# A graph layer's message sums: three more batches of edges through dense counts, 23 fewer gathered groups

## The chip, the core and the metric

The kernel runs on one core of one Trainium2 chip. The metric is the device time of one execution in microseconds; the median of three runs of the kernel before is 1320.35 us (1319.23 to 1321.12).

## What is computed

One message-passing layer on 6250 nodes with 128 features and 206250 edges sorted by destination, each with one of three types:

```
h = relu(layernorm(x))
parts = [relu(h)]
for t in range(3):
    msg = relu(h[src] @ W_e[t].T + b_e[t])
    msg = where(edge_type == t, msg, 0)
    parts.append(segment_sum(msg, dst, 6250))
agg = concatenate(parts, axis=1)
for t in range(3):
    updated = where(node_type == t, agg @ W_n[t].T + b_n[t], updated)
out = x + updated + h
```

## The kernel before

**Table.** Messages depend on the source node and the type alone. So the first stage (up to about 78 us) computes, for each of 49 tiles of 128 nodes, all three messages of each node (`mm`, L705 and L707) and writes them to a table in HBM. What is left is a sum of table rows for each destination. Two ways of doing that run side by side.

**Gathered groups.** The first `E0` edges are cut into `GD` groups of 512. POOL fetches a group's 512 table rows by four indirect DMAs of 128 rows (L647) into one of six slots. VectorE builds a one-hot of destination and type (L1205), TensorE multiplies the rows by it (L770, four f32 matmuls of 27 columns, each two passes in the profile), and VectorE adds the sums to the accumulator `acc` (L1297). Groups are taken from the last to the first, one in each step.

**Dense batches.** The last `NW` = 2 × `BATCHES` rows of 1920 edges (15 tiles of 128) are not gathered. For each type and batch (`q` runs over 3 × `BATCHES` passes; a batch is two rows) TensorE first counts how often each source node occurs for each of 64 destination columns. That is a *build*: `count` (L791) multiplies one-hots of a source's low 7 bits (`lhot`, `lmid`, L1230 and L1225) by one-hots of its high bits and the destination column (`jhot`, `jmid`, L1216). A row's 15 tiles are done in three builds (`UNITS`), in seven pieces of the columns (`CUT`), each in a PSUM bank that ScalarE casts to f16 into `counts` (L957). Of 15 tiles, `D_OFF` gives the first column of each and `D_WID` its number of columns; a tile's destinations must lie in this window. A *product* (L807) then multiplies the counts by the table of that type, split into three bf16 parts ("planes"): seven products of seven 384-column matmuls for each pass. VectorE sums the three parts (L1318), TensorE transposes (L814), VectorE adds to `acc` (L1297).

**Finish.** A tile of 128 nodes whose sums are complete is multiplied by the node weights (L825 to L829) and stored.

**Order.** The steps are laid out when the kernel is built. `dealt` deals out builds and products evenly, by `SIZE` (3 for a product, 2, 2 and 3 for the builds, 9 for a finish), over steps 1 to `NS` − 7, where `NS` is the number of gathered groups. In each step TensorE does the gathered group, a finish if one is due, then its share of dense pieces. VectorE prepares the one-hots of step s + 1 in step s. POOL runs up to six groups ahead.

**What else the change touches.** `LEAD` rows ahead of the dense ones are loaded with them so that the number of rows is a multiple of 16 (L504), and are marked as empty (`far(e_typ)` in the POOL block). `SPLIT` gives the step at which each of seven groups of planes of the first type is split into its parts (`load_planes`, `plane_top`, `plane_rest`, `plane_low`); the products of that type wait for them. If any edge lies outside its window, `flag` is set and a branch at the end of the kernel recomputes all sums.

Of the kernel before, what the change touches and what calls it, by code (L numbers as in the profile page):

```python
# [24 lines left out]
PAD_SRC = 2666666  # L25
PAD_TYPE = -T * PAD_SRC

BATCHES = 23
BW = 2
WT = 15  # L30
WE = WT * P
LEAD = 2
SLOTS = 6
OFF = (0, 3, 9, 11)
WID = (8, 8, 7, 9)
WS = 9
MID = 9
WG = 20
D_OFF = (0, 4, 9, 13, 17, 21, 25, 29, 33, 37, 40, 44, 48, 51, 55)
D_WID = (9, 9, 7, 7, 7, 7, 6, 6, 6, 7, 8, 7, 8, 9, 9)  # L40
D_WS = 9
D_MID = 27
D_AT = (0, 7, 12)
ROUND = 12582912.0
SL = 64
CUT = (0, 10, 20, 29, 39, 48, 56, 64)
UNITS = ((0, 1), (2, 3), (4, 5, 6))
OWN = ((0, 1, 2, 3), (5, 6, 7, 8), (10, 11, 12, 13, 14))
CROSS = (4, 9)
# [13 lines left out]
def build(nc, x, src, dst, etype, ntype, w_e, b_e, w_n, b_n, out):  # L63
# [9 lines left out]
    TD = T * D  # L73
    NW = BATCHES * BW
    E0 = E - NW * WE
    LR = LEAD + NW
    GD = -(-E0 // GE)
    NS = GD
    SF = E0 // GE
    SR = E0 - SF * GE  # L80
    PIECES = len(CUT) - 1
    NQ = T * BATCHES
    NA = LEFT + NB * P + SL
# [8 lines left out]
    assert D == P and NR and ER and GF == G - 1 and NB == MC * 7 and NB == HB  # L92
    assert SF == GD - 1 and SR and LR <= HALF and LR % 16 == 0 and BW * SL <= 128 and max(D_WID) == D_WS and WT % 2 == 1
    assert HB * max(z - a for a, z in zip(CUT, CUT[1:])) <= 512 and CUT[-1] == SL
    assert 5 * EW <= T * NA and EW % 4 == 0 and OFF[-1] + WS == WG and D_OFF[-1] + D_WS == SL and T * JT < 2048
    assert LEFT >= D_MID and SLOPE * G * 1.0 <= N and P < GD <= 2 * P
# [10 lines left out]
    def group_at(s):  # L107
        return NS - 1 - s
# [31 lines left out]
    def touches(g, i):  # L140
        return SLOPE * g - SLACK - MID <= (i + 1) * P - 1 and SLOPE * g + AHEAD + WG > i * P

    def wide_touches(w, i):
        first = SLOPE / TPG * (E0 // P + w * WT)
        return first - SLACK - D_MID <= (i + 1) * P - 1 and first + AHEAD + SL > i * P


    def plan(hand):
        at = {i: s for s in range(D0, D1 + 1) for kind, i in hand[s] if kind == "prod"}
        last = [at[q * MC + MC - 1] for q in range(NQ)]  # L150
        wide_done = [last[NQ - BATCHES + w // BW] + 2 for w in range(NW)]
        ready = [max([s for s in range(NS) if touches(group_at(s), i)] + [wide_done[w] for w in range(NW) if wide_touches(w, i)])
# [46 lines left out]
        return [j for j in range(NB) if FIN[j] == s]  # L199


    SPLIT = (-1, -1, -1, 0, 0, 0, 2)

    def splits_at(s):
        return [m for m in range(MC) if SPLIT[m] == s]


    def kept_step(k):
        t, c = divmod(k, MC)
        a, z = (PROD_STEP[t * BATCHES * MC] if t else SPLIT[-1]) + 5, PROD_STEP[((t + 1) * BATCHES - 2) * MC]  # L210
        return a + (z - 6 - a) * c // (MC - 1)

    KEEP = [kept_step(k) for k in range((T - 1) * MC)]
    FETCH = [PROD_STEP[((k // MC + 1) * BATCHES - 1) * MC + k % MC] for k in range((T - 1) * MC)]

# [6 lines left out]
    with ExitStack() as ctx:  # L222
        def sb(name, shape, dt=F32):
            return ctx.enter_context(nc.sbuf_tensor(name, shape, dt))
# [18 lines left out]
        def far(a):  # L243
            return a[:, ES:EW]
# [10 lines left out]
        KEPT = [u for own in OWN for u in own]  # L255
        JW = HB * sum(D_WID[u] for u in KEPT)
        JAT = {u: HB * sum(D_WID[v] for v in KEPT if v < u) for u in KEPT}
        JB = max(AB, NB * D)
# [6 lines left out]
        lhot = sb("lhot", [P, len(KEPT), P], BF16)  # L265
        jmid = {u: sb(f"jmid{u}", [P, 2, HB * D_WID[u]], BF16) for u in CROSS}
        lmid = {u: sb(f"lmid{u}", [P, 2, P], BF16) for u in CROSS}
# [15 lines left out]
        col_s = sb("col_s", [1, -(-GD // 4) * 4], I32)  # L283
        col_d = sb("col_d", [1, BATCHES, 4], I32)
        flag = sb("flag", [1, 4], I32)
# [175 lines left out]
        def wide_keys(to, m):  # L461
            n = 2 * TPG
            b = (m - PAIR) // 2
            return (to[:, :, b * n:(b + 1) * n].rearrange("p w (c h) -> p c h w", h=2),
                    psE[m % 2][:, :].rearrange("p (c h w) -> p c h w", h=2, w=HALF)[:, :, :, LEAD:LR])

        def bank_of(i, p):
            return i // 3 * PIECES + p
# [8 lines left out]
        def _(sp):  # L477
# [20 lines left out]
            def dense_tiles(e0):  # L498
                return e0[E0 - LEAD * WE:E].rearrange("(w u j) -> w u j", u=WT, j=P)

# [104 lines left out]
        def _(pool):  # L605
# [10 lines left out]
                      allow_small_or_imprecise_dtypes=True).then_inc(consts, 1)  # L616
            pool.iota(bound[:, SB_:GB], [[0, 1]], base=E0 // P - LEAD * WT, channel_multiplier=WT,
                      allow_small_or_imprecise_dtypes=True).then_inc(consts, 1)
# [8 lines left out]
            for h in range(2):  # L627
                pool.memset(far(e_typ)[h * HALF:h * HALF + LEAD, :], PAD_TYPE).then_inc(lead_ok, 1)
                pool.wait_ge(lead_ok, h + 1)
# [43 lines left out]
        def _(pe):  # L673
# [101 lines left out]
            def hots(i, u):  # L775
                if u in CROSS:
                    return lmid[u][:, i // 3 % 2, :], jmid[u][:, i // 3 % 2, :]
                return lhot[:, KEPT.index(u), :], jhot[:, JAT[u]:JAT[u] + HB * D_WID[u]]

            def count(i):  # L780
                pe.wait_ge(dhot_ok, i + 1)
                for p in UNITS[i % 3]:
                    m = bank_of(i, p)
                    if m >= 3:
                        pe.wait_ge(d_count, m - 2)
                    low, high = CUT[p], CUT[p + 1]
                    tiles = [u for u in range(WT) if D_OFF[u] < high and D_OFF[u] + D_WID[u] > low]
                    for u in tiles:
                        a, z = max(D_OFF[u], low), min(D_OFF[u] + D_WID[u], high)
                        rows_hot, cols_hot = hots(i, u)  # L790
                        t = pe.matmul(psB[m % 3][:, HB * (a - low):HB * (z - low)], rows_hot,  # L791
                                      cols_hot[:, HB * (a - D_OFF[u]):HB * (z - D_OFF[u])],
                                      start=(u == tiles[0]), stop=(u == tiles[-1]), skip_group_check=True)
# [84 lines left out]
        def _(act):  # L878
# [70 lines left out]
            def counted(i):  # L949
# [3 lines left out]
                for p in UNITS[i % 3]:  # L953
                    m, n = bank_of(i, p), CUT[p + 1] - CUT[p]
                    a = k // 3 * SL + CUT[p]
                    act.wait_ge(d_build, m + 1)
# [86 lines left out]
        def _(dve):  # L1043
# [14 lines left out]
            for h in range(2):  # L1058
                for n in range(WC):
                    u = min(2 * n + h, WT - 1)  # L1060
                    dve.memset(off_v[h * HALF:(h + 1) * HALF, n:n + 1], float(D_OFF[u]))
                    m = dve.memset(wid_v[h * HALF:(h + 1) * HALF, n:n + 1], float(D_WID[u]))
# [175 lines left out]
            def take_low():  # L1238
                dve.wait_ge(turn_t, LOW + 1)
                got = psE[LOW % 2]  # L1240
                dve.tensor_scalar(col_s[:, 0:GD], got[0:1, 0:GD], float(LEFT), None, ALU.add)
                dve.tensor_scalar(col_d[:, :, 0:BW], got[0:1, SB_ * P + LEAD:SB_ * P + LR].rearrange("p (b k) -> p b k", k=BW),
                                  float(LEFT), None, ALU.add).then_inc(turn_d, 1)
# [224 lines left out]
```

## Time and profile before

| | |
|---|---|
| median of 3 runs | 1320.35 us |
| span of the profiled execution | 1595.0 us |
| TensorE busy (matmuls) | 1392.9 us, 87% |
| VectorE busy | 1114.8 us, 70% |
| POOL busy | 920.6 us, 58% |
| ScalarE busy | 584.8 us, 37% |
| DMA, mean | 76 GB/s |
| granted TensorE clock, mean | 0.927 |

The profiled execution took 275 us longer than the median of the runs. The page gives for each group of instructions the summed busy time, the mean duration of one, and the idle time of the engine before them with what ended it. Matmuls are pipelined: the duration of one (339 ns for 384 columns) is longer than the distance between two starts, so distances are read from the timeline.

### The profile page before, as it was taken

Reading aid. Unit: us, or ns where it says so; the run is one execution under the profiler, and the core shown is the slowest. Engines: PE = TensorE matmul, PEld = TensorE weight load, DVE = VectorE, ACT = ScalarE, POOL = GpSimd, SP = SyncE. Lnnn points to the kernel's source line nnn. Section 1 sums busy time; section 2 is a strip of 40 time slices with the busy share of each in tenths; the row PEclk is TensorE's granted clock in tenths of the full one; section 3 lists DMA queues with packets and bytes.
Section 4 is the critical chain, followed back from the end, with each engine's and each line's share of the span. In section 5 each row is a group of like instructions: output and inputs, shape, how many; then the busy total and the mean of one; then the engine's idle time right before and its main releaser. Section 6 shows DMA issues by size and latency. Waiting matters only on the chain.

```text
span 1595.0 us, 26681 instructions
## 1 busy us (share of the span) xinstructions
PE 1392.9 (87%) x9175; PEld 946.5 (59%) x9175; DVE 1114.8 (70%) x3845; ACT 584.8 (37%) x1165; POOL 920.6 (58%) x979
## 2 busy tenths in 40 slices
PE   7867998998999988898989888988797898888898
PEld 3544665666666656566666566656565565655565
DVE  8786887777878786777777676865565566555542
ACT  6753443433443433343334333432232223222220
POOL 3376666665666665655665565665555565555552
PEclk9978999998999999999999899999998899888989
DMA  9652222122222531222222223321211121111211
GB/s 283 215 136 54 74 72 78 49 74 72 77 50 61 170 88 47 76 60 57 76 79 58 54 65 110 101 54 50 55 45 50 50 52 49 50 47 49 54 46 37
DMA packets 97259, 120.60 MB, mean 76 GB/s; under 512 B 19947, under 2 KB 77170, under 8 KB 97124
## 3 DMA queue, kind: packets, MB, share of 16 engines
q0 software_dynamic: 29568, 60.61, 15.2%
q1 hardware_dynamic: 67078, 58.03, 11.8%
q8 instruction: 75, 1.23, 0.3%
q14 instruction: 60, 0.49, 0.1%
q10 hardware_dynamic: 478, 0.23, 0.0%
HBM read 93.12 MB, written 25.68 MB: 74 GB/s over the span
## 4 chain that ended last, share of the span: by engine, by line
PE 78%; another core or an unknown queue 6%; issue 6%; DVE 6%; ACT 3%; SPq 1%; DMA 0%; DVEq 0%; ACTq 0%
PE ps L807 33%; PE ps L791 23%; PE ps L770 12%; PE ps L829 6%; ACT arena L957 2%; PE ps L826 2%; DVE arena L1216 1%; DVE lhot L1230 1%; PE ps L707 1%; PE ps L814 1%; PE ps L825 1%; DMA acc<-in_dst_dram 0%; DVE work L1323 0%; DVE stats L1088 0%
## 5 line engine op out<-in xcount | busy, mean ns | idle before, releaser
L647 POOL DMA_INDIRECT rows<-message_table,idx x924 | 893.9, 967 | 601.8 <-PE ps L770 239.9
L957 ACT CAST arena<-ps 128x490 f16<-128x490 f32 (+2 forms) x966 | 495.5, 566 | 924.3 <-PE ps L791 585.0
L807 PE MATMUL ps<-mem,arena 128*128 128x384 bf16 x3381 | 659.1, 339 | 12.7 <-DVE mem L1328 6.4
L1216 DVE TENSOR_SCALAR arena<-iota_j,jkey 128x441 bf16<-128x441 f16 (+3 forms) x1794 | 465.8, 324 | 182.8 <-PE ps L791 113.8
L791 PE MATMUL ps<-arena,lhot 128*128 128x294 bf16 (+8 forms) x2622 | 398.2, 284 | 155.4 <-ACT arena L957 78.8
L807 PEld LDWEIGHTS ps<-mem,arena 128*128 128x128 f16 x3381 | 333.6, 103 | 225.8 <-issue 48.0
L791 PEld LDWEIGHTS ps<-arena,lhot 128*128 128x128 bf16 x2622 | 218.8, 102 | 270.7 <-issue 137.8
L1230 DVE TENSOR_TENSOR lhot<-ps,lkey 128x512 bf16<-128x512 f32 (+1 forms) x412 | 297.2, 721 | 0.0
L1297 DVE TENSOR_TENSOR acc<-ps,acc 128x60 f32 (+1 forms) x369 | 80.3, 218 | 267.7 <-PE ps L770 138.0
L770 PEld LDWEIGHTS ps<-onehot,rows 128*128 128x128 f32 x1848 | 250.1, 205 | 18.0 <-issue 8.1
L770 PE MATMUL ps<-onehot,rows 128*128 128x27 f32 x1848 | 244.1, 274 | 4.6 <-DVE acc L1297 4.0
L791 PE MATMUL ps<-jmid,lmid 128*128 128x147 bf16 (+3 forms) x552 | 134.9, 245 | 8.2 <-issue 5.1
L829 PE MATMUL ps<-wnT,acc 128*128 128x384 f32 x294 | 112.3, 521 | 0.4 <-issue 0.2
L829 PEld LDWEIGHTS ps<-wnT,acc 128*128 128x128 f32 x294 | 60.6, 206 | 46.6 <-issue 10.8
L1216 DVE TENSOR_SCALAR jmid<-iota_j,jkey 128x343 bf16<-128x343 f16 x276 | 85.1, 308 | 0.0
L791 PEld LDWEIGHTS ps<-jmid,lmid 128*128 128x128 bf16 x552 | 61.1, 111 | 34.7 <-issue 7.9
L1225 DVE TENSOR_TENSOR lmid<-ps,lkey 128x128 bf16<-128x128 f32 x274 | 76.4, 279 | 0.0
L1205 DVE TENSOR_TENSOR onehot<-ps,key 128x108 f32<-128x108 f32 x231 | 59.2, 256 | 0.0
L1346 DVE SCALAR_TENSOR_TENSOR xr<-ps,mask,xr 128x128 f32<-128x128 f32 x147 | 51.0, 347 | 4.8 <-PE ps L829 1.4
L826 PE MATMUL ps<-wnT,work 128*128 128x384 f32 x98 | 43.7, 528 | 0.4 <-issue 0.4
L707 PE MATMUL ps<-weT,work 128*128 128x384 f32 x96 | 39.5, 493 | 3.4 <-ACT work L906 3.4
L1318 DVE TENSOR_REDUCE slots<-ps 128x128 f32<-128x384 f32 x69 | 37.6, 545 | 0.0
(129 smaller groups left out, 412.6 us busy)
## 6 DMA issues: line engine op xcount, KB each, us to landing
rows<-message_table,idx POOLq DMA_INDIRECT x924
work<-message_table SPq DMA_DIRECT2D x21, 448.0 KB
kept_planes<-work SPq DMA_DIRECT2D x14, 672.0 KB
mem<-kept_planes SPq DMA_DIRECT2D x14, 672.0 KB
message_table<-work SPq DMA_DIRECT2D x25, 192.0 KB, 2.1
message_table<-rows SPq DMA_DIRECT2D x24, 192.0 KB, 2.0
own_hT<-work SPq DMA_DIRECT2D x49, 64.0 KB, 1.8
work<-own_hT SPq DMA_DIRECT2D x49, 64.0 KB
```

The costliest lines, as they stand in the source:

```text
L647: pool.indirect_dma_start(out=rows[:, s % SLOTS, u, :], out_offset=None, in_=table_rows, in_offset=bass.IndirectOffsetOnAxis(ap=idx[:, gro ...
L770: m = pe.matmul(to[:, :, OFF[u]:OFF[u] + WS], rows[:, s % SLOTS, u, :], onehot[:, s % 4, u, :].rearrange("p (t w) -> p t w", t=T), start=( ...
L791: t = pe.matmul(psB[m % 3][:, HB * (a - low):HB * (z - low)], rows_hot, cols_hot[:, HB * (a - D_OFF[u]):HB * (z - D_OFF[u])], start=(u == ...
L807: m = pe.matmul(psQ[q % 2][0:BW * SL, 0:3 * D], counts[q % 2][:, c * MC + e, :], planes[:, c * MC + e, :, :].rearrange("p v d -> p (v d)") ...
L826: pe.matmul(to[:, 0:TD], hT_own[:, j % 4, :], wnT[:, 0, :], start=False, stop=False)
L829: m = pe.matmul(to[:, 0:TD], nodes[:, t, i * P:(i + 1) * P], wnT[:, 1 + t, :], start=False, stop=(t == T - 1))
L957: act.copy(counts[q % 2][:, :, a:a + n], psB[m % 3][:, 0:HB * n].rearrange("p (w h) -> p h w", w=n)).then_inc(d_count, 1)
L1205: dve.tensor_tensor(onehot[:, s % 4, :, :], iota_b, key[:, group_at(s), :].unsqueeze(2).to_broadcast(shape), ALU.is_equal).then_inc(hot_ok, 1)
L1216: dve.tensor_scalar(to, iota_j[:, 0:HB * D_WID[u]], float(t * JT), jkey[:, w, u:u + 1], ALU.add, ALU.is_equal)
L1225: dve.tensor_tensor(lmid[u][:, i // 3 % 2, :], numbers, lkey[:, w, u:u + 1].to_broadcast([P, P]), ALU.is_equal)
L1230: dve.tensor_tensor(lhot[:, at:at + n, :], numbers.unsqueeze(1).to_broadcast(full), lkey[:, w, u:u + n].unsqueeze(2).to_broadcast(full), A ...
L1297: dve.tensor_tensor(there, sums_, there, ALU.add).then_inc(acc_add, 1)
```

## The change

Three more batches of dense edges (26 for 23, so 52 rows for 46) take 11520 edges from the gathered part, which has 208 groups instead of 231. Twelve lead rows instead of two make 64 loaded rows. Tile 9 covers columns 36 to 43 (was 37 to 43), tile 12 columns 47 to 55 (was 48 to 55); the piece boundary at 48 moves to 47. The last group of planes is split at step 1 instead of 2.

```
-BATCHES = 23
+BATCHES = 26
 BW = 2
 WT = 15
 WE = WT * P
-LEAD = 2
+LEAD = 12
...
-D_OFF = (0, 4, 9, 13, 17, 21, 25, 29, 33, 37, 40, 44, 48, 51, 55)
-D_WID = (9, 9, 7, 7, 7, 7, 6, 6, 6, 7, 8, 7, 8, 9, 9)
+D_OFF = (0, 4, 9, 13, 17, 21, 25, 29, 33, 36, 40, 44, 47, 51, 55)
+D_WID = (9, 9, 7, 7, 7, 7, 6, 6, 6, 8, 8, 7, 9, 9, 9)
...
-CUT = (0, 10, 20, 29, 39, 48, 56, 64)
+CUT = (0, 10, 20, 29, 39, 47, 56, 64)
...
-    SPLIT = (-1, -1, -1, 0, 0, 0, 2)
+    SPLIT = (-1, -1, -1, 0, 0, 0, 1)
```

## Rows read from the trace of the kernel before

**Rows 1.** The page, part 1: busy us (share of span) x instructions.

```profile
PE 1392.9 (87%) x9175; PEld 946.5 (59%) x9175; DVE 1114.8 (70%) x3845; ACT 584.8 (37%) x1165; POOL 920.6 (58%) x979
```

**Rows 2.** Windows: start:end length, busy of each engine (x), PEclk, DMA share, GB/s.

```profile
78.00:140.00 62.00, 37.90 (x205) 23.57 (x206) 44.82 (x123) 29.22 (x46) 45.95 (x43) 0.70 0.43 110
140.00:1570.00 1430.00, 1271.44 (x8623) 874.93 (x8621) 1001.05 (x3459) 501.50 (x962) 847.98 (x882) 0.93 0.24 65
```

**Rows 3.** The page, part 4: the chain that ended last, by engine.

```profile
PE 78%; another core or an unknown queue 6%; issue 6%; DVE 6%; ACT 3%; SPq 1%; DMA 0%; DVEq 0%; ACTq 0%
```

**Rows 4.** Waits: who waited for whom, us in total, times, longest.

```profile
ACT arena L957 <- PE ps L791: 585.0, 336, 9.9
POOL rows L647 <- PE ps L770: 239.9, 95, 7.7
...
PE ps L791 <- ACT arena L957: 79.3, 31, 6.4
```

**Rows 5.** Timeline of TensorE in a steady stretch: start us, us, what.

```profile
142.93 0.27 PE L814 MATMUL ps<-ident,slots 128*128 128x128 f32 x1
143.04 0.97 PE L770 MATMUL ps<-onehot,rows 128*128 128x27 f32 x8
143.85 0.84 PE L791 MATMUL ps<-arena,lhot 128*128 128x441 bf16 x6
...
144.59 1.30 PE L807 MATMUL ps<-mem,arena 128*128 128x384 bf16 x7
145.73 0.25 PE L791 MATMUL ps<-jmid,lmid 128*128 128x196 bf16 x1
...
146.40 1.30 PE L807 MATMUL ps<-mem,arena 128*128 128x384 bf16 x7
147.54 0.97 PE L770 MATMUL ps<-onehot,rows 128*128 128x27 f32 x8
148.35 0.27 PE L791 MATMUL ps<-jmid,lmid 128*128 128x245 bf16 x1
...
149.32 2.44 PE L807 MATMUL ps<-mem,arena 128*128 128x384 bf16 x14
```

**Rows 6.** Timeline at the end: a finish of TensorE and its last matmuls.

```profile
1578.27 0.32 PE L825 MATMUL ps<-bn_all,ones 128*128 128x384 bf16 x1
...
1581.01 0.97 PE L770 MATMUL ps<-onehot,rows 128*128 128x27 f32 x8
...
1589.72 2.10 PE L829 MATMUL ps<-wnT,acc 128*128 128x384 f32 x6
```

**Rows 7.** Timeline of TensorE: the first build.

```profile
77.98 0.84 PE L791 MATMUL ps<-arena,lhot 128*128 128x441 bf16 x6 [2.26 <-DVEq L1286]
```

**Rows 8.** Timeline of POOL: its first indirect DMA and its last two.

```profile
78.30 1.10 POOL L647 DMA_INDIRECT rows<-message_table,idx  x1 [6.56 <-DMA message_table<-work]
...
1565.27 0.94 POOL L647 DMA_INDIRECT rows<-message_table,idx  x1 [0.30 <-issue]
1566.52 0.94 POOL L647 DMA_INDIRECT rows<-message_table,idx  x1 [0.30 <-issue]
```

**Rows 9.** The page, part 5: groups of a row's dense work, busy us, mean ns.

```profile
L957 ACT CAST arena<-ps 128x490 f16<-128x490 f32 (+2 forms) x966 | 495.5, 566 | 924.3 <-PE ps L791 585.0
...
L1216 DVE TENSOR_SCALAR arena<-iota_j,jkey 128x441 bf16<-128x441 f16 (+3 forms) x1794 | 465.8, 324 | 182.8 <-PE ps L791 113.8
...
L1230 DVE TENSOR_TENSOR lhot<-ps,lkey 128x512 bf16<-128x512 f32 (+1 forms) x412 | 297.2, 721 | 0.0
...
L1216 DVE TENSOR_SCALAR jmid<-iota_j,jkey 128x343 bf16<-128x343 f16 x276 | 85.1, 308 | 0.0
...
L1225 DVE TENSOR_TENSOR lmid<-ps,lkey 128x128 bf16<-128x128 f32 x274 | 76.4, 279 | 0.0
```

**Rows 10.** The page, part 3: the DMA queue of SP, packets, MB, share of 16 engines.

```profile
q1 hardware_dynamic: 67078, 58.03, 11.8%
```

**Rows 11.** Waits: a product of TensorE for the planes' last part.

```profile
PE ps L807 <- DVE mem L1328: 6.4, 1, 6.4
```

## The prediction

> **What bounds the kernel now.** I read the busy shares first, then the windows, the chain, one steady stretch of TensorE, and last who waits for whom. TensorE is busy 1392.9 of 1595.0 us, VectorE 1114.8, POOL 920.6 and ScalarE 584.8 [rows 1]. From 140 to 1570 us the order is the same [rows 2], and 78% of the chain that ended last is TensorE [rows 3]. The waits agree: ScalarE waits 585.0 us for the count matmuls and POOL 239.9 us for the gathered ones, while TensorE waits 79.3 us for ScalarE [rows 4]. So the others wait for TensorE.
>
> One thing must be settled before anything is summed: the profiled execution took 1595.0 us and the median of the runs is 1320.35. A busy share of a pipelined engine doesn't say how much of the 275 us is slack, so I priced TensorE by the distance from the start of one group to the start of the next, where it never stops [rows 5]:
> - a product (seven matmuls of 384 columns): 145.73 − 144.59 = 1.14 us;
> - a dense row's three builds: 0.74 (143.85 to 144.59), 0.67 (145.73 to 146.40) and 0.97 (148.35 to 149.32), together 2.38 us;
> - a gathered group (eight f32 passes): 148.35 − 147.54 = 0.81 us;
> - a transpose of the sums: 143.04 − 142.93 = 0.11 us;
> - a finish: 1581.01 − 1578.27 = 2.74 us [rows 6].
>
> TensorE without one stall, before: 77.98 us until the first build [rows 7], 69 × 7 × 1.14 = 550.6, 138 rows × 2.38 = 328.4, 231 × 0.81 = 187.1, 49 × 2.74 = 134.3, 69 × 0.11 = 7.6, and 3.2 us behind the last matmul (it ends at 1591.8, the span at 1595.0 [rows 6]). That is 1289.2 us. The profiled execution is 305.8 us above it, by pauses and half-clock stretches (the granted clock is 0.93 from 140 to 1570 us, 0.70 from 78 to 140 [rows 2], of full 2.4 GHz). The median is only 31 us above it. So in the runs that are timed TensorE is all but saturated, and what the profile shows as slack of TensorE is not there to be filled. This is the step on which all else rests. I take the 31 us for the start of the dense work above all: from 78 to 140 us TensorE is busy 37.9 of 62.0 us [rows 2], waiting for planes, one-hots and the first sums.
>
> **The change part by part.** The dense rows go from 46 to 52, the dense tail of the edge list from 88320 to 99840 edges, the gathered groups from 231 to 208. Each batch is done once for each of three edge types, so batch passes go from 69 to 78.
> - Products: 9 × 7 × 1.14 = +71.8 us on TensorE, on the path.
> - Builds: 18 more passes over a row × 2.38 = +42.8 us.
> - Wider tiles: tile 9 has 8 columns instead of 7 and tile 12 has 9 instead of 8. A row's builds stream 49 columns more for each, 5586 for 5488, in 24 matmuls for 23, since the cut moves from 48 to 47 and tile 10 now reaches into the sixth piece. By the 384-column price (1.14 / 7 = 0.163 us) 98 columns are 0.042 us, with one more issue about 0.05; × 156 rows = +7.8 us.
> - Transposes: 9 × 0.11 = +1.0 us.
> - Gathered groups: 23 × 0.81 = −18.6 us. That is all that TensorE gets back: a group of 512 edges costs it 0.81 us, while a batch of 3840 edges (7.5 groups, 6.1 us gathered) costs 3 × (7 × 1.14 + 2 × 2.38 + 0.11) = 38.6 us dense. Dense work pays only where POOL is the bound.
> - POOL: one indirect DMA each 1.25 us [rows 8], four a group, so 23 × 5.0 = 115 us less. Before, 924 × 1.25 = 1155 us, from 78.3 us to 1233 at its own pace, plus 27.5 us from its last to the end of the span [rows 8]: 1261, some 60 us under the median. POOL is not the bound, so these 115 us are worth nothing, or at most a part of the 31 us.
> - VectorE: a row's one-hots take (465.8 + 85.1 + 297.2 + 76.4) / 138 = 6.7 us busy, an upper end since neighbours overlap [rows 9]; × 18 = 121 us. With the rest nearly even (27 more sums and adds, 46 fewer one-hots and adds of groups), 1114.8 + 121 = 1236 busy. That is 84% of 1320 before and 87% of 1426 after: beside TensorE's work, but closer. ScalarE adds 18 × 7 casts × 0.566 = 71 us [rows 9] to 584.8: 46% of the time, hidden. If that cover were gone, VectorE's own excess would show: see the second rival.
> - Start: the lead goes from 2 to 12 rows, so the dense load reads 64 rows instead of 48, of 15 tiles each, for three arrays: 720 more packets of 512 bytes, against 23 shorter rows of groups. VectorE needs them all before it can work on edges. The queue's 67078 packets took 11.8% of 16 engines' 1595 us, 0.045 us each [rows 10]; 720 over 16 engines are +2.0 us, less some for the shorter rows: I take +1.5, ends 0 (the landing is hidden) and 4 (twice the estimate).
> - The planner: a step's share of dense work rises from 12.5 to 15.5 of its units, over 201 steps instead of 224, and the seventh group of planes is split one step earlier, since its product comes in the first half of step 3. In the trace of before one product waits 6.4 us for such planes [rows 11]; ends −4 and +4 us, value 0. SP issues the load of these planes one step earlier, and nothing is queued behind it but the next x tile.
>
> Sum: 71.8 + 42.8 + 7.8 + 1.0 − 18.6 + 1.5 = +106.3 us. TensorE without a stall goes to 1289.2 + 106.3 = 1395.5. With the same 31 us of stalls the time is 1320.35 + 106.3 = 1426.6, and I say **1426 us**, 8% more. Against the profiled execution's own time, stalls come with work: the stretch between the first build and the last matmul is 1208 us of work in 1513.8, so the span should grow by 106.3 × 1.25 = 133 us, to about 1728. The same ratio, 1.083, on the median gives 1430.
>
> By the Trainium skill (TensorE: Matmul & The Clock Gate, Back-to-back issue gap) a lone matmul's gap is N/2.4 + 2.5 ns, which for 384 columns is 162.5 ns: the trace's 1.14 / 7 = 0.163 agrees. The same section gives sustained pairs of weight load and matmul 131 ns at 512 columns and 81 at 128; by an estimate between the two, some 114 ns at 384, the 3822 products would take 187 us less, and the sum above would be a fall. No row here shows such a spacing.
>
> **The rivals.**
> 1. *Stalls shrink too.* If the 31 us are POOL's doing in part (1261 of 1320 leaves it 60 us, less in steps with little dense work), the larger steps hide them. 1395.5 is the end of that: 1396 to 1410. For it: POOL's waits for TensorE are the longest but one. Against it: those are waits of POOL, not for POOL.
> 2. *VectorE becomes the bound in dense steps.* It is at 0.87 of the time on average by an upper price. If an eighth to a third of the 121 us that its 18 row passes add shows (16 to 44 us), the time is 1442 to 1470. Against it: VectorE waits for count matmuls and for gathered sums, and 78% of the chain is TensorE.
> 3. *Faster: TensorE in the timed runs is quicker than its spacing in the trace, and POOL sets the pace.* Then the 23 groups bring 23 × 5.0 = 115 us and the time is 1205. This decides from the point where TensorE's 1395.5 us shrink below 1320, that is by 5.4% or more in spacing. For it: the 275 us between profile and median aren't explained by a row. Against it: 0.163 us for 384 columns is 2.36 columns a ns at a full granted clock, and the median lies above the sum, not below. The skill's 131 ns for sustained pairs (same page and section) would be this rival; the trace speaks against it.
> 4. *The change doesn't do what it says:* an edge of the new rows falls outside a window, and the kernel redoes everything in its branch for leftover edges: 403 groups × 49 blocks, each 8 passes of 384 columns at about 0.3 us (a finish does nine in 2.74 us [rows 6]), some 50 ms. Counting the reference's edges against the windows, with the old widths one of the 52 rows has edges outside (11 of them) and with the new ones none, so this hardly stands.
>
> **How the numbers follow.** Forecast 1426 (1410 to 1442): 0.86. Rival 1: 0.04, rival 2: 0.05, rival 3: 0.03, rival 4: 0.02. The low end takes half of the 31 us away, the high end adds 13% to TensorE's waits for ScalarE (79 × 0.13 = 10, as builds grow from 138 to 156) and the upper ends of start and planner. The other cases outside it hold about 0.14, and a few hundredths of the forecast's own lie beyond its ends. A measurement tells about 0.2% from no change. Faster by more: 0.03, all of rival 3; within 0.2%: 0.01, its edge; slower by more: 0.96.
>
> **What would show it.** In the profile after: 3822 products and 3744 count matmuls, 832 indirect DMAs, 208 gathered groups of 0.81 us; product spacing still 1.14 us and a row's builds 2.43; the span near 1728 with the granted clock about 0.93. POOL's waits for TensorE should grow from 239.9 to well over 300 us, since each step now has some 7 us of TensorE work and 5.0 of gathering. TensorE's waits for VectorE should stay under some 20 us; if they grow to 50, it is rival 2. The prediction is wrong if the median rises by much less than 100 us: then TensorE was not saturated in the timed runs, and the sum of 1289 is not a floor.

## The result, and the profile after

The changed kernel takes 1437.16 us in the median of 4 runs (1435.86 to 1438.97), the kernel before 1320.73 in the same comparison: a ratio of 1.088 (95% interval 1.087 to 1.090), or 116.4 us more, where the forecast was 1426 and the range 1410 to 1442.

The profiled execution of the changed kernel took 1434.1 us, close to its median; that of the kernel before, on which the prediction had to rest, took 1595.0. So the two profiles can't be compared. Experiment e0 gave a profile of the kernel before in which it runs as it does in the timed runs, with a span of 1318.5 us. The page's first lines of the changed kernel, columns as in [rows 1]:

```profile
span 1434.1 us, 28779 instructions
PE 1390.1 (97%) x10011; PEld 971.1 (68%) x10011; DVE 1217.8 (85%) x4186; ACT 653.2 (46%) x1291; POOL 839.8 (59%) x887
PE 81%; DVE 13%; SPq 2%; ACT 2%; issue 1%; DMA 1%; DVEq 0%; ACTq 0%
```

The same lines of the kernel before, from e0:

```profile
span 1318.5 us, 26681 instructions
PE 1282.3 (97%) x9175; PEld 908.3 (69%) x9175; DVE 1109.0 (84%) x3845; ACT 573.0 (43%) x1165; POOL 931.5 (71%) x979
PE 89%; DVE 5%; ACT 1%; SPq 1%; DMA 1%; issue 1%; DVEq 0%; ACTq 0%
```

TensorE is busy for 97% of either span: 107.8 us more of it, and a span that is 115.6 us longer. VectorE's part of the chain that ended last went from 5% to 13%: the first sign of what the sum lacked.

A steady stretch of TensorE in the changed kernel, to be set beside [rows 5] (start us, us, what):

```profile
132.62 0.84 PE L791 MATMUL ps<-arena,lhot 128*128 128x441 bf16 x6
...
133.37 1.30 PE L807 MATMUL ps<-mem,arena 128*128 128x384 bf16 x7
134.50 0.25 PE L791 MATMUL ps<-jmid,lmid 128*128 128x196 bf16 x1
...
135.19 1.30 PE L807 MATMUL ps<-mem,arena 128*128 128x384 bf16 x7
136.32 0.27 PE L814 MATMUL ps<-ident,slots 128*128 128x128 f32 x1
136.43 0.97 PE L770 MATMUL ps<-onehot,rows 128*128 128x27 f32 x8
137.25 0.27 PE L791 MATMUL ps<-jmid,lmid 128*128 128x245 bf16 x1
...
138.24 2.44 PE L807 MATMUL ps<-mem,arena 128*128 128x384 bf16 x14
```

A product is 134.50 − 133.37 = 1.13 us, a row's three builds are 0.75 + 0.69 + 0.99 = 2.43, a gathered group is 137.25 − 136.43 = 0.82, a transpose 0.11. All prices of the sum hold to 0.01 us for each piece of work (e1 has more on the widened row).

Where the rest of the time is shows in the windows, first of e0 and then of the changed kernel (columns as in [rows 2]):

```profile
78.00:140.00 62.00, 47.42 (x307) 33.06 (x306) 56.05 (x164) 34.86 (x59) 48.59 (x45) 0.78 0.41 112
...
200.00:900.00 700.00, 698.62 (x5281) 503.63 (x5280) 628.08 (x2169) 318.18 (x622) 518.66 (x530) 1.00 0.29 89
900.00:1280.00 380.00, 379.71 (x2669) 270.61 (x2669) 293.69 (x1039) 134.22 (x270) 280.21 (x293) 1.00 0.23 66
```

```profile
78.00:140.00 62.00, 46.59 (x292) 31.28 (x292) 57.24 (x168) 35.28 (x58) 44.74 (x44) 0.75 0.44 123
...
200.00:900.00 700.00, 691.37 (x5274) 491.09 (x5275) 635.61 (x2169) 337.91 (x642) 419.83 (x426) 1.00 0.26 72
900.00:1280.00 380.00, 379.63 (x2731) 267.85 (x2730) 311.55 (x1088) 151.75 (x294) 230.28 (x240) 1.00 0.24 66
```

From 78 to 140 us TensorE idles 14.6 us before and 15.4 after, at a granted clock of 0.78 and 0.75 of full speed. From 200 to 900 us it idles 1.4 us before; after the change, 8.6 us, and almost nothing later, where VectorE is 82% busy instead of 90.8%. So the steady part has some 7 us of stalls that it didn't have. VectorE's share in that stretch was 89.7% before, hardly less.

The waits of the changed kernel, to be set beside [rows 4] (us in total, times, longest):

```profile
ACT arena L957 <- PE ps L791: 673.5, 443, 6.3
POOL rows L647 <- PE ps L770: 321.0, 196, 3.2
...
DVE arena L1216 <- PE ps L791: 109.0, 115, 2.7
...
ACT work L978 <- DVE work L1333: 31.8, 14, 3.4
...
PE ps L791 <- ACT arena L957: 8.7, 9, 2.1
```

VectorE's waits for a free one-hot were 41.1 us in e0: it idles more than before at one point of its order and is late at another. Where it is late shows in the fourth line. The planes of types two and three are split ahead of their use (the *kept* planes): VectorE subtracts the top part (L1333), ScalarE casts what is left (L978), VectorE subtracts again (L1337). ScalarE does its work in a fixed order, so while it waits for L1333, the casts of counts behind it (L957) wait too. These waits were 16.4 us in e0, the longest 2.7. One of the changed kernel's stalls (timeline):

```profile
349.74 1.08 DVE L1333 TENSOR_TENSOR work<-work 128x896 f32<-128x896 f32 x1
...
350.85 0.94 ACT L978 CAST work<-work 128x896 bf16<-128x896 f32 x1 [2.94 <-DVE work L1333]
...
351.70 2.06 ACT L957 CAST arena<-ps 128x490 f16<-128x490 f32 x4
...
352.32 0.47 PE L791 MATMUL ps<-arena,lhot 128*128 128x98 bf16 x3 [0.96 <-ACT arena L957]
```

Of TensorE's 8.6 us of idle time from 200 to 900 us, 6.2 come like this, in seven stalls, each within 2.2 us behind the start of a cast L978 that had waited for L1333. All of e0's 1.4 us do too.

### The profile page after: what moved, and what is told of

The parts are those of the page before. It is cut to its first block, busy times and chain, and to the rows that moved or that the text cites. A ratio compares the mean times of both kernels' runs of the same rounds, so it can differ in the third digit from the quotient of the medians.

```text
span 1434.1 us, 28779 instructions
## 1 busy us (share of the span) xinstructions
PE 1390.1 (97%) x10011; PEld 971.1 (68%) x10011; DVE 1217.8 (85%) x4186; ACT 653.2 (46%) x1291; POOL 839.8 (59%) x887
## 4 chain that ended last, share of the span: by engine, by line
PE 81%; DVE 13%; SPq 2%; ACT 2%; issue 1%; DMA 1%; DVEq 0%; ACTq 0%
PE ps L807 37%; PE ps L791 23%; PE ps L770 10%; PE ps L829 7%; DVE arena L1216 5%; DVE lhot L1230 3%; PE ps L826 2%; PE ps L707 1%; DVE jmid L1216 1%; DVE xr L1346 1%; DVE lmid L1225 1%; DVE work L1333 1%; PE ps L814 1%; PE ps L825 1%; ACT arena L957 1%
## 5 line engine op out<-in xcount | busy, mean ns | idle before, releaser
L647 POOL DMA_INDIRECT rows<-message_table,idx x832 | 813.1, 977 | 522.5 <-PE ps L770 321.0
L957 ACT CAST arena<-ps 128x490 f16<-128x490 f32 (+2 forms) x1092 | 563.4, 588 | 673.8 <-PE ps L791 673.5
L807 PE MATMUL ps<-mem,arena 128*128 128x384 bf16 x3822 | 701.3, 327 | 1.8 <-DVE acc L1297 1.0
L1216 DVE TENSOR_SCALAR arena<-iota_j,jkey 128x441 bf16<-128x441 f16 (+3 forms) x2028 | 528.9, 324 | 109.6 <-PE ps L791 109.0
L807 PEld LDWEIGHTS ps<-mem,arena 128*128 128x128 f16 x3822 | 365.1, 99 | 217.8 <-issue 9.0
L1230 DVE TENSOR_TENSOR lhot<-ps,lkey 128x512 bf16<-128x512 f32 (+1 forms) x466 | 335.4, 720 | 0.0
L770 PEld LDWEIGHTS ps<-onehot,rows 128*128 128x128 f32 x1664 | 209.0, 193 | 13.2 <-issue 5.1
L770 PE MATMUL ps<-onehot,rows 128*128 128x27 f32 x1664 | 205.2, 264 | 4.4 <-DVE acc L1297 4.3
L791 PE MATMUL ps<-jmid,lmid 128*128 128x147 bf16 x624 | 151.8, 244 | 6.2 <-DVE lhot L1230 6.2
L1216 DVE TENSOR_SCALAR jmid<-iota_j,jkey 128x343 bf16<-128x343 f16 (+1 forms) x312 | 96.2, 308 | 0.0
```

Of the source, the lines that this page charges most:

```text
L647: pool.indirect_dma_start(out=rows[:, s % SLOTS, u, :], out_offset=None, in_=table_rows, in_offset=bass.IndirectOffsetOnAxis(ap=idx[:, gro ...
L770: m = pe.matmul(to[:, :, OFF[u]:OFF[u] + WS], rows[:, s % SLOTS, u, :], onehot[:, s % 4, u, :].rearrange("p (t w) -> p t w", t=T), start=( ...
L807: m = pe.matmul(psQ[q % 2][0:BW * SL, 0:3 * D], counts[q % 2][:, c * MC + e, :], planes[:, c * MC + e, :, :].rearrange("p v d -> p (v d)") ...
L957: act.copy(counts[q % 2][:, :, a:a + n], psB[m % 3][:, 0:HB * n].rearrange("p (w h) -> p h w", w=n)).then_inc(d_count, 1)
L1216: dve.tensor_scalar(to, iota_j[:, 0:HB * D_WID[u]], float(t * JT), jkey[:, w, u:u + 1], ALU.add, ALU.is_equal)
L1230: dve.tensor_tensor(lhot[:, at:at + n, :], numbers.unsqueeze(1).to_broadcast(full), lkey[:, w, u:u + n].unsqueeze(2).to_broadcast(full), A ...
```

## The experiments

**e0: the kernel before again.** No edit.

> The kernel before, unchanged. Theory (TensorE is saturated in the timed runs; the 306 us of pauses and half clock in the profiled execution belong to that execution): another profiled execution has a span near 1319 us, the granted clock near 0.99, and TensorE's distances of 1.14 us for a product, 2.38 for a row's builds and 0.81 for a gathered group unchanged. Rival (the pauses come from being profiled): the span is again near 1595 us while the timed runs stay at 1320.

Measured: 1320.97 us in 10 runs, ratio 0.999 (0.998 to 1.000), span 1318.5 us at a mean granted clock of 0.99. The prices are those of [rows 5]. The theory holds so far: the 306 us of pauses and half clock in the profiled execution of before don't belong to profiling as such, and not to the runs that gave the median. What they do belong to, the last section takes up. TensorE's sum of 1289 us lies 29 us under this span. From 78 to 140 us it idles 14.6 us, and the clock of 0.78 costs up to 0.22 × 62 = 13.6 us there; from 140 to 1280 it idles 1.7 us in all. So nearly all of the 29 us are the start, where the prediction put its 31.

**e1: the wider tiles alone.**

```diff
-D_OFF = (0, 4, 9, 13, 17, 21, 25, 29, 33, 37, 40, 44, 48, 51, 55)
-D_WID = (9, 9, 7, 7, 7, 7, 6, 6, 6, 7, 8, 7, 8, 9, 9)
+D_OFF = (0, 4, 9, 13, 17, 21, 25, 29, 33, 36, 40, 44, 47, 51, 55)
+D_WID = (9, 9, 7, 7, 7, 7, 6, 6, 6, 8, 8, 7, 9, 9, 9)
-CUT = (0, 10, 20, 29, 39, 48, 56, 64)
+CUT = (0, 10, 20, 29, 39, 47, 56, 64)
```

> The kernel before with the wider tiles 9 and 12 and the cut at 47 alone, still 23 batches. Theory: 138 rows x 0.05 us more of TensorE, +6.9 us, 1327.6 us. If TensorE still has slack in the timed runs, the time stays at 1320. If VectorE or ScalarE is near the bound, their wider one-hots and casts add to it: 10 us or more.

Measured: 1327.03 us beside 1322.39 of the kernel before, ratio 1.0033 (1.0021 to 1.0045), so +4.4 us (2.8 to 5.9). The wider tiles cost something, as they would where TensorE has no slack, but a third less than the 6.9 us of the sum. The traces show about half of the difference: by the medians of the distances a row's first build takes the same in e0 and e1, the second 0.667 and 0.686 us, the third 0.974 and 0.997. That is 0.042 us a row, the price of the 98 columns; the 24th matmul adds nothing. Over 138 rows it makes 5.8 us. The rest lies within the interval.

**e2: more loaded rows alone.**

```diff
-LEAD = 2
+LEAD = 18
```

> The kernel before with 18 lead rows instead of 2, so that 64 rows are loaded as in the changed kernel; nothing else. Theory: the edges land later by 1.5 us (0 to 4), and the first build, at 77.98 us in the kernel before and 81.59 in the changed one, moves by as much: 1322 us. If the later first build of the changed kernel comes from another thing, it stays at 78 us here and the time at 1320.

Measured: 1324.19 us beside 1322.39, ratio 1.0012 (1.0003 to 1.0021), so +1.6 us (0.4 to 2.8), as expected from the sum's 1.5. In the profiled execution the first build starts at 82.16 us, against 77.41 in e0:

```profile
82.16 1.29 PE L791 MATMUL ps<-arena,lhot 128*128 128x441 bf16 x6 [2.23 <-DVEq L1286]
```

```profile
77.41 1.47 PE L791 MATMUL ps<-arena,lhot 128*128 128x441 bf16 x6 [2.23 <-DVEq L1286]
```

That is 4.7 us in one execution. Of the kernels that ran where the kernel before takes 1321 us, those with 48 loaded rows had it between 77.41 and 80.17 us, and those with 64 rows between 80.05 and 83.35. The means are 3.2 us apart, but the groups overlap, so a single profile is no measure of this term, and the timed ratio is the better one.

**e3: one batch fewer than before.**

```diff
-BATCHES = 23
+BATCHES = 22
-LEAD = 2
+LEAD = 4
```

> 22 batches and 4 lead rows with the old windows: one batch fewer than the kernel before, 238 gathered groups for 231. Theory (TensorE alone sets the pace): 3 x 12.85 us less of dense work and 7 x 0.81 us more of gathered: -32.9 us, 1288 us. Rival (POOL takes over): POOL's own pace is 78.3 + 952 x 1.25 + 27.5 = 1296 us, so the time stops falling there, 1296 to 1306 us. If POOL already sets the pace at 23 batches, the time rises by 7 x 5 = 35 us to 1355.

Measured: 1311.16 us beside 1322.39, ratio 0.992 (0.990 to 0.995). It is faster than the kernel before by 0.5 to 1.0%, some 10 us, and than the changed kernel by some 126. TensorE alone would have given 1288, and even the rival's range ended at 1306. Its waits show who came last:

```profile
POOL rows L647 <- issue: 284.7, 934, 0.3
...
PEld ps L770 <- DMA rows<-message_table,idx: 16.9, 17, 2.3
...
PE ps L770 <- DMA rows<-message_table,idx: 10.7, 12, 2.1
```

POOL waits 5.2 us for TensorE in all (60.8 us in e0), and TensorE waits for gathered rows, 12 times. So POOL gathers nearly without a pause and is already the last at 22 batches. The span of 1305.5 us is its first DMA at 79.1 us, 951 distances of 1.279 us in the mean, and 10.1 us behind the start of the last; TensorE's sum with e0's 29 us of stalls would give 1286. The point of equal time lies between 22 and 23 batches.

**e4: two batches fewer than before.** The edit of e3 with 21 batches and 6 lead rows.

> 21 batches, 6 lead rows, old windows, 246 gathered groups. Theory (below 23 batches POOL sets the pace, 1.25 us for each indirect DMA): 78.3 + 984 x 1.25 + 27.5 = 1336 us, more than the 1311 us of 22 batches and the 1321 of 23. If it was only the fewer dense batches that made 22 faster, the time falls on, by 33 us more, to 1278.

Measured: 1349.92 us, ratio 1.021 (1.019 to 1.022). POOL sets the pace, as the chain says:

```profile
POOL 63%; issue 21%; PE 10%; DVE 3%; DMA 1%; ACT 1%; SPq 0%; POOLq 0%; DVEq 0%; ACTq 0%
```

The 14 us over 1336 are two misses that in part cancel. The profiled span of 1352.6 us is 80.7 us up to the first indirect DMA, 983 distances of 1.282 us in the mean (1.25 is their median), and 11.8 us behind the start of the last, where the expectation took 27.5.

**e5: one batch more than before, with the new windows.**

```diff
-BATCHES = 26
+BATCHES = 24
-LEAD = 12
+LEAD = 16
```

(against the changed kernel)

> 24 batches, 16 lead rows, the changed kernel's windows, 223 groups. Theory (TensorE's sum with nothing new): 1320.7 + 38.6 dense - 8 x 0.81 gathered + 144 x 0.05 for the wider tiles + 2 to 4 us at the start = 1362 to 1364 us. Rival (stalls grow with each batch, VectorE near its bound): part of the changed kernel's extra stalls show already, 1366 to 1371 us.

Measured: 1359.87 us beside 1321.53, ratio 1.029 (1.028 to 1.031). That is 2 to 4 us less than TensorE's sum, not more (by the ratio +38.9 us, where the sum has 41 to 43), and from 200 to 900 us TensorE is busy 699.8 of 700:

```profile
200.00:900.00 700.00, 699.83 (x5363) 503.74 (x5362) 637.83 (x2183) 334.20 (x633) 483.71 (x494) 1.00 0.30 86
```

So the rival falls for 24 batches: no new stalls yet, though VectorE is 91.1% busy there. From 24 to 26 batches the sum gives 2 × 38.9 − 15 × 0.81 = 65.6 us, and 77.3 were measured: the whole excess arises in these last two batches.

**e6: half of the gathering.** In the kernel before:

```diff
-                for u in range(TPG):
+                for u in range(TPG if s < SLOTS else 2):
                     pool.indirect_dma_start(
...
-                pe.wait_ge(landed[s % SLOTS], 16 * TPG * (s // SLOTS + 1))
+                pe.wait_ge(landed[s % SLOTS], 16 * TPG + 32 * (s // SLOTS))
```

> The kernel before, but from the seventh gathered group on POOL fetches only two of a group's four tiles of rows (the other two matmuls use old rows, so those messages are left out); every other instruction stays. POOL's indirect DMAs fall from 924 to 474. Theory (POOL has slack at 23 batches, so its saving is worth nothing): 1318 to 1321 us, no change. Rival 1 (some of TensorE's 31 us of stalls come from POOL): 1290 to 1312 us.

Measured: ratio 0.9996 (0.9987 to 1.0006), with POOL busy 503.0 us instead of 931.5. Rival 1 falls, and the 115 us of gathering that the change takes away were worth nothing. The first six groups were gathered whole here; for them e0's waits tell: from 78 to 140 us TensorE waits 14.6 us, for VectorE and ScalarE, and never for gathered rows. So none of the 29 to 31 us above TensorE's sum is POOL's.

**e7: less VectorE work in the changed kernel.**

```diff
-                for u in OWN[kind]:
+                for u in (OWN[kind] if i < 6 else OWN[kind][:2]):
                     column_hot(jhot...
```

> The changed kernel, but from the seventh build on VectorE writes only the first two of a build's own three, four or five column one-hots and leaves out the rest (so counts are taken from old one-hots, that part of the computation is left out); TensorE, ScalarE and POOL do all as before. VectorE does some 1.5 us less for each row, 235 us in all. Theory (8 to 10 us of the changed kernel's stalls between 200 and 900 us are VectorE's): 1426 to 1430 us. Rival (those stalls are ScalarE's casts, since TensorE's rows name them as what it waits for): 1436 to 1438 us.

(A build has four, four or five one-hots of its own.) Measured: 1421.35 us, 15.8 less than the changed kernel (1437.16; the two ran beside kernels before of 1321.5 and 1320.7 us), and more of a gain than the 7 to 11 us that were expected. VectorE is busy 986.5 us instead of 1217.8. From 200 to 900 us TensorE is now busy 699.4 of 700:

```profile
200.00:900.00 700.00, 699.39 (x5354) 498.67 (x5353) 511.17 (x1574) 342.33 (x650) 413.39 (x432) 1.00 0.26 73
```

The new stalls are gone, so they come from VectorE's work, though the waits name ScalarE's casts. For the most part the way goes through the kept planes' splits, as the rows above show: with less VectorE work in front of them, ScalarE's longest wait for L1333 falls from 3.4 to 1.9 us. Where the 15.8 us are shows when the same product matmul starts in the two traces. The changed kernel is 2.0 us behind at the first (105.2 and 103.1 us), of which 1.5 are the first build, ahead of the edit; 5.0 behind at the 201st (172.1 and 167.1); 15.2 at the 2401st (884.7 and 869.5); and 15.9 at the last. So 10 us are the stretch from 172 to 885 us (TensorE's busy time has 8.0 of them), some 5 are the start, and next to nothing is behind them. How much of that the kernel before would also gain was to be told by e8.

**e8: the same cut in the kernel before.** The edit of e7.

> The kernel before with the same cut of VectorE's work as in e7_less_vector (from the seventh build on only the first two of a build's own column one-hots are written; that part of the computation is left out). Of the 15.8 us that e7 gave on the changed kernel, theory says some 5 us are the start, which both kernels have, and some 10 us are VectorE's share of the steady part, which only the changed kernel has: here 1314 to 1318 us. Rival (VectorE costs the same in both and explains nothing of the difference): 1304 to 1308 us.

Measured: 1593.89 us beside 1591.88 of the kernel before, ratio 0.999 (0.995 to 1.003). The last four kernels ran on another chip, on which the kernel before itself takes 1577 to 1608 us in 23 runs, and the profile looks like that of [rows 1] to [rows 3]: TensorE is busy 87% of the span and 79% of the chain. Neither value that was expected can be read from it. For the steady part e0's trace answers: TensorE idles 1.7 us there from 140 to 1280 us, so the kernel before has no more than that to gain, and 8 to 10 us are the changed kernel's own. What the cut gives at the start, at 1320 us, stays open.

**e9: six of seven product matmuls, in the kernel before.**

```diff
-                for e in range(MC):
+                for e in (0, 1, 2, 3, 4, 6):
                     m = pe.matmul(psQ...
```

> The kernel before with six instead of seven matmuls in each product (a seventh of the products' sum is left out), 483 x 0.163 = 78.7 us less of TensorE. If TensorE alone sets the pace: 1242 us. Theory (POOL takes over on the way, with 924 indirect DMAs at 1.25 to 1.27 us from 78 us on and 27 us behind them): 1261 to 1280 us.

Measured on that chip: 1604.2 us, ratio 1.005 (1.001 to 1.009). A cut of 79 us in TensorE's work brings nothing there, even a little loss. The trace shows a pause that isn't any engine's work (timeline):

```profile
357.52 2.11 PE L807 MATMUL ps<-mem,arena 128*128 128x384 bf16 x12
...
360.90 0.95 POOL L647 DMA_INDIRECT rows<-message_table,idx  x1 [0.30 <-issue]
362.86 0.57 ACT L957 CAST arena<-ps 128x441 f16<-128x441 f32 x1 [8.01 <-remote]
363.54 0.32 PEld L791 LDWEIGHTS ps<-arena,lhot 128*128 128x128 bf16 x3 [4.30 <-issue]
363.57 1.41 PE L791 MATMUL ps<-arena,lhot 128*128 128x441 bf16 x6 [3.94 <-issue]
```

The count matmuls for which ScalarE waits have started before 357.52, and the products behind them end at 359.6; ScalarE goes on at 362.86. TensorE then stands for 3.94 us, most likely for the cast (the profile names no releaser), and its next six count matmuls take 1.41 us where 0.84 is usual [rows 5]. The expectation of 1261 to 1280 us can't be tested on this chip.

**e10: the same cut in the changed kernel.** The edit of e9.

> The changed kernel with six instead of seven matmuls in each product (a seventh of the products' sum is left out), 546 x 0.163 = 89.0 us less of TensorE. POOL is far off the bound here (832 x 1.26 + 105 = 1153). If TensorE alone sets the pace: 1348 us. Theory (VectorE, at 85% of the changed kernel's time, is so near that it shows more when TensorE shrinks): 1352 to 1375 us.

Measured on that chip: 1459.15 us in 4 runs (1443.67 to 1465.69), beside 1591.88 of the kernel before: ratio 0.913 (0.905 to 0.921). Neither 1348 nor 1352 to 1375: this chip doesn't tell the two apart.

**e11: small splits of the kept planes in the changed kernel.**

```diff
-dve.tensor_tensor(raw[:, :, :], raw[:, :, :], made[:, :, 0, :], ALU.subtract)
+dve.tensor_tensor(raw[:, 0:1, :], raw[:, 0:1, :], made[:, 0:1, 0, :], ALU.subtract)
...
-dve.tensor_tensor(made[:, :, 2, :], raw[:, :, :], made[:, :, 1, :], ALU.subtract)
+dve.tensor_tensor(made[:, 0:1, 2, :], raw[:, 0:1, :], made[:, 0:1, 1, :], ALU.subtract)
```

> The changed kernel with the 28 subtractions that split the kept planes (L1333 and L1337, 1.0 us each) done on one of seven tiles only (the planes of types two and three are wrong in the rest, that part is left out). VectorE does some 24 us less, all before 900 us, where the changed kernel's steady stalls are. Theory (the stalls come where VectorE is over 90% busy, and the splits push it there): 1428 to 1432 us. Rival (the stalls come from the dense share of each step alone): 1436 to 1438 us.

Measured on that chip: 1459.82 us, ratio 0.917 (0.913 to 0.921). Neither 1430 nor 1437, so the time doesn't decide. The trace says something: the first subtraction takes 0.28 us instead of 1.08, and yet, of 10.8 us of TensorE's idle time from 200 to 900 us, 5.6 still come right behind a cast L978 that had waited for L1333. So it doesn't look as if the length of the subtractions made the stalls; rather the point in VectorE's order at which the split stands. On the chip of 1320 us no run tests that. e10 has 89 us less of TensorE than e11 and the same time, so on this chip these kernels too are held by something else. The changed kernel itself was not run there. But e11 leaves out only 24 us of VectorE's work of it, and takes 132 us less than the kernel before. So it is likely, though not shown, that the change is a gain on that chip and the loss of 9% is one of chips on which the kernel before takes 1320 us.

## Why the prediction was right

- *TensorE is all but saturated in the timed runs, whatever the profiled execution shows.* Right, and the step on which all rested: e0's span lies 29 us above the stall-free sum, where the profile of before lay 306 above it, and nearly all of the 29 are the start, as foretold. They hardly grew with the change (14.6 and 15.4 us idle from 78 to 140). The way there, distances between starts times counts, set against the median and not against the span, is what carried the forecast.
- *Products, builds, transposes, gathered groups.* Right to 0.01 us each. The changed kernel's trace has the 3822 product matmuls, 3744 count matmuls and 832 indirect DMAs that were foretold.
- *Wider tiles, +7.8 us over 156 rows.* A little too high: 0.042 us a row and not 0.05, since the added matmul costs nothing beside its columns, so 6.5 us. Alone and over 138 rows they cost 4.4 instead of 6.9.
- *Start, +1.5 us (0 to 4).* Right by the timed e2 (1.6), though the profiled first build moved by 4.2 us (77.41 to 81.59).
- *The planner, value 0.* No run has the earlier split of the seventh group alone. In e0 TensorE waits 1.9 us for such planes, in the changed kernel not at all, so its part is small.
- *POOL's 115 us are worth nothing.* Right (e6). POOL's waits for TensorE grew to 321.0 us, as foretold, and from 60.8 in e0 rather than 239.9.
- *VectorE's 121 us are hidden.* This is the term that was mis-sized. VectorE's busy time grew by 109 us (1109.0 to 1217.8). It was judged by its share, 87%, and set to nothing, and 8 to 10 us of it show, between 172 and 885 us (e7, less at most 1.7 that the kernel before has too). The share alone could not have told: from 200 to 900 us it is 89.7, 91.1 and 90.8% at 23, 24 and 26 batches, and only the last has the stalls. The rows show the way that most of it takes: VectorE comes late to a kept plane's split, ScalarE stands for it up to 3.4 us, the casts of counts behind it come late, and TensorE waits for a free bank. Why this starts between 24 and 26 batches is an argument and not shown by a run: a step then mostly holds six dense pieces instead of four or five, and VectorE has its one-hots to do ahead of the split.
- *Rival 2.* It named the engine, and its 16 us or more came as 8 to 10. (An eighth to a third of 121 us is 15 to 40, not 16 to 44.)
- *Rivals 3 and 4.* The spacing of product matmuls is 162 ns in both kernels, and the time rose, so rival 3 falls. The changed kernel's trace ends at 1434.1 us without the branch for leftover edges, so rival 4 falls.
- *The range, 1410 to 1442.* It held, and by luck in its upper part. Its 10 us for TensorE's waits for ScalarE were worked out from the 79.3 us of the disturbed execution; in e0 these waits are 3.8 us, and in the changed kernel 8.7. That these 10 us are about as large as what VectorE brought in has no reason behind it.
- *The span near 1728 us with a clock of 0.93.* Wrong: 1434.1 and 0.988. It took the ratio of one disturbed execution (stalls that come with work, × 1.25) for a property of the kernel. The same ratio on the median (1430) did no harm.
- *TensorE's waits for VectorE stay under 20 us.* As read from the waits that holds (6.2 us for the one-hots), and it was the wrong sign to look for: VectorE's lateness shows as a wait of ScalarE for VectorE, as one of TensorE for ScalarE's casts, and in the chain.

In the two profiled executions the excess over the sum is 115.6 − 106.3 = 9.3 us: 2.7 at the start (4.2 for 1.5), within what single profiles scatter, and 6.6 behind it. By the medians it is 10.1. With the wider tiles at 6.5 us it is 1.3 more in either case. Behind the start that makes 7.9 us in the profiles, which is what VectorE's 8 to 10 us account for.

The sum also says where the best number of batches lies. A batch costs TensorE 38.6 us and saves it 6.1, and saves POOL 7.5 groups of 5.1 us (four DMAs of 1.28), some 38 us. So more batches pay only while POOL is last: 1350, 1311, 1321, 1360 and 1437 us for 21, 22, 23, 24 and 26 batches (the last two with the wider tiles and 64 loaded rows). The version with 22 beats both kernels, the kernel before by 0.8%.

## What to carry to other kernels

Where work can go one of two ways over two engines, price one unit of it on each engine by distances between starts; time falls only while work leaves the engine that is last, and the best split is where both take equal time (here between 22 and 23 batches, with TensorE's 12.85 us a pass against POOL's 5.1 us a group). Set the sum against the timed runs before reading slack from a profile: the 306 us by which one profiled execution lay above the sum were not there in them. And an engine at 90% in the steady stretch, given more work to hide, is worth a charge of its own: its share doesn't tell whether its order of work still fits. Look where another engine waits for it in a fixed order, since all that stands behind such a wait is late too.

## What the runs showed that was not expected

On one chip the same kernel took 1592 us (23 runs), on two others 1321 to 1322. The profile of before, which the prediction had, fits the first: its span of 1595.0 us and its clock of 0.927 lie among those of that chip's 23 runs (1576 to 1606 us, 0.924 to 0.939), and none of the runs on the two others came near. So it was most likely taken on such a chip, while the median of 1320 was not; no run tells which chip it was. In the slow profiles the usual distances are the same (median 162 ns for a 384-column matmul), but there are pauses, nearly all of 1 to 6 us (one of 19 in e8), in which ScalarE, VectorE and POOL go on only some us after the matmuls that they wait for are over, and TensorE then waits for them. It looks as if the end of the matmuls reached them late, which isn't shown. Gaps of over 0.9 us between matmul starts number 84 with 203 us in e8, against 12 with 26 us in e0. The granted clock falls to 0.935 (e8) and 0.907 (e9), from 0.99. Taking 79 us from TensorE (e9) or half of the builds' own one-hots from VectorE (e8) brought nothing there, while e10 and e11, which have 208 gathered groups in place of 231, take 133 and 132 us less. Over the groups, (1592 − 105) / 231 = 6.4 us and (1459 − 105) / 208 = 6.5 us are alike, which would fit a pace tied to the gathering or to its signals; no run tells that from other causes, and it stays open.
